# Causal masks of an attention layer: added on TensorE, or on VectorE and GpSimd

## What is computed

```python
q = (x @ wq).reshape(B, T, 2, 4, 128)          # T = 2048, 2 key groups, 4 heads each
k = einsum('bkhl,ld->bkhd', k_lat, wk_up)
scores = einsum('bqhrd,bkhd->bhrqk', q, k) * scale
scores = where(causal, scores, finfo.min)       # causal = tril(ones(T, T))
probs = softmax(scores, axis=-1)
y = einsum('bhrqk,bkhd->bqhrd', probs, v) @ wo
x = layernorm(x + y)                            # then a quantised FFN, a second
                                                # (full) attention, a mixture of experts
```

## Time and profile before

| | |
|---|---|
| median of 3 runs | 1496.16 us (1495.47 to 1496.18) |
| the profiled execution | 1495.46 us, its span 1493.7 us |
| busy: PE, DVE, ACT, POOL | 1341.5, 1087.3, 847.7, 72.0 us |
| mean granted TensorE clock | 0.924 of full speed |
| layer 0 and its FFN | from about 28 to 640 us of the span |
| layer 1 | from about 640 us to the end |

### The profile page before, as it was taken

How to read it: one execution, slowest core, us unless ns; L and a number is a source line. 1 busy time by engine, 2 the same in 40 slices (tenths; PEclk the granted TensorE clock), 3 DMA queues, 4 the chain that set the end, 5 groups by cost and what they waited for, 6 DMA issues and landing times.

```text
span 1493.7 us, 19302 instructions
## 1 busy us (share of the span) xinstructions
PE 1341.5 (90%) x6597; PEld 580.2 (39%) x6597; DVE 1087.3 (73%) x2165; ACT 847.7 (57%) x1621; POOL 72.0 (5%) x99
## 2 busy tenths in 40 slices
PE   5789899989999975789999999999999999999894
PEld 3444445344443432433333333333333333333332
DVE  3677587578644577778888788888789887987323
ACT  2445534564555421167777666777566776677660
POOL 2000000000000000000000002000011000000033
PEclk8678899899999986589999999999999999999897
DMA  3000000000000000000000000000000000000000
GB/s 100 1 1 1 1 1 1 1 1 1 1 0 1 0 1 0 0 1 1 1 1 1 1 1 8 2 1 1 1 1 8 1 1 2 1 1 1 1 7 8
DMA packets 8865, 6.19 MB, mean 4 GB/s; under 512 B 2168, under 2 KB 8128, under 8 KB 8768
## 3 DMA queue, kind: packets, MB, share of 16 engines
q1 hardware_dynamic: 8768, 4.97, 1.2%
HBM read 3.72 MB, written 1.05 MB: 3 GB/s over the span
## 4 chain that ended last, share of the span: by engine, by line
PE 72%; DVE 15%; ACT 7%; issue 3%; POOL 1%; DMA 1%; SPq 1%; DVEq 0%; POOLq 0%; ACTq 0%
PE ps L755 24%; PE ps L738 16%; PE ps L654 8%; DVE MP L1150 8%; PE ps L734 6%; PE ps L660 4%; ACT PR L932 4%; PE ps L650 2%; PE ps L719 2%; PE ps L668 1%; PE ps L686 1%; ACT QO L831 1%; PE ps L619 1%; PE ps L697 1%; POOL qc L1001 1%
## 5 line engine op out<-in xcount | busy, mean ns | idle before, releaser
L1150 DVE TENSOR_REDUCE MP<-ps 128x1 f32<-128x512 f32 (+2 forms) x1344 | 822.4, 664 | 175.8 <-PE ps L654 94.1
L932 ACT ACTIVATE PR<-ps 128x512 f32<-128x512 f32 (+2 forms) x1344 | 700.7, 586 | 438.4 <-PE ps L738 231.9
L755 PE MATMUL ps<-PR,V 128*32 128x512 f32 (+2 forms) x2688 | 438.6, 610 | 0.6 <-ACT OS L831 0.5
L738 PE MATMUL ps<-Q,KO 64*128 64x512 f32 x1024 | 364.6, 469 | 29.7 <-ACT PR L932 20.3
L654 PE MATMUL ps<-KO,Q 64*128 64x512 f32 x1024 | 353.5, 448 | 17.1 <-DVE MP L1150 12.8
L738 PEld LDWEIGHTS ps<-Q,KO 64*128 64x128 f32 x1024 | 154.9, 188 | 353.5 <-ACT PR L932 289.4
L654 PEld LDWEIGHTS ps<-KO,Q 64*128 64x128 f32 x1024 | 164.5, 192 | 82.9 <-DVE MP L1150 47.4
L734 PE MATMUL ps<-QO,KO 97*128 97x512 f32 (+3 forms) x320 | 148.5, 475 | 19.2 <-ACT PR L932 17.1
L660 PE MATMUL ps<-KO,QO 96*128 96x512 f32 (+2 forms) x320 | 137.2, 466 | 15.7 <-DVE QO L1131 12.6
L755 PEld LDWEIGHTS ps<-PR,V 128*32 128x32 f32 (+1 forms) x2688 | 74.3, 116 | 124.1 <-ACT PR L932 66.5
L734 PEld LDWEIGHTS ps<-QO,KO 97*128 97x128 f32 x320 | 63.6, 203 | 146.4 <-ACT PR L932 89.4
(11 more groups left out here) (180 smaller groups left out, 762.7 us busy)
## 6 DMA issues: line engine op xcount, KB each, us to landing
Q<-MR SPq DMA_DIRECT2D x64, 2.0 KB
result<-V SPq DMA_DIRECT2D x4, 256.0 KB, 2.3
H<-in_L_attn_wq SPq DMA_DIRECT2D x1, 512.0 KB, 6.9
HQT<-in_L_attn_wo SPq DMA_DIRECT2D x1, 512.0 KB, 4.9
ew<-in_L_ffn_expert_w SPq DMA_DIRECT2D x1, 512.0 KB
const<-in_consts SPq DMA_DIRECT2D x1, 197.0 KB, 2.3
bq<-in_L_attn_bq SPq DMA_DIRECT2D x12, 0.1 KB
wd<-in_L_ffn_w_down SPq DMA_DIRECT2D x1, 176.0 KB, 3.6
```

What stands on the lines that cost most here:

```text
L738: m = nc.tensor.matmul(dst[:, :], KO1[rows, g, kt * P:(kt + 1) * P], Q1[rows, it, h // 2, :], start=True, stop=True)
L755: nc.tensor.matmul(dst, VO[layer][:, kt, g, :], PR[:, u % NP_RING, q0:QC], start=kt == 0, stop=kt == key_tiles(layer, c) - 1).then_inc(pv_ ...
L932: nc.scalar.activation(PR[:, u % NP_RING, q0:QC], ps[:, 8 - nb + u % nb, q0:QC], ACT.Exp, scale=SCALE[layer]).then_inc(exp_done, 1)
L1150: v.tensor_reduce(MP[:, buf, h, q, kc:kc + 1], bank[:, 0:w], AX, ALU.max).then_inc(free, 1)
```

## The change

- The two mask matmuls (lines 663 and 740) are gone: 128 of each. The matmul before each now closes the bank.
- A diagonal maximum is now one `tensor_tensor_reduce` of VectorE: it adds `mask_qk` (now 512 wide, zeros and then the triangle, bf16) to the bank, writes the sum back into the bank, and keeps the maximum. The other 1216 maxima stay as they were.
- The exponents of a diagonal slot are computed unmasked. GpSimd then sets the part above the diagonal to zero in `PR` (`affine_select`, 128 by 128, in place), and the products of that slot wait for GpSimd (`clipped`) instead of ScalarE.
- The table `const` loses both masks; the one mask left comes by a DMA of its own, into `qa`, and VectorE converts it.
- The step list isn't cut any more: one walk over the whole program, with three pads at its very end, and no seam.

```diff
+        def diagonal(layer, c, kt):
+
+            return layer == 0 and kt >= c * QT
...
-            walk(part0, Count([]), 0)
-            walk(first1, n0, 0)
-            for c in range(1, NC - 1):
-                walk(padded(steps1(c, False, False)), start_of(c), HG)
-            walk(padded(steps1(NC - 1, False, True)), start_of(NC - 1), HG)
+            walk(program, Count([]), 0)
...
-            sp.dma_start(const[:, :], A["consts"]).then_inc(ld["const"], 16)
+            sp.dma_start(const[:, :], A["consts"][:, 0:CONST_W]).then_inc(ld["const"], 16)
+            sp.dma_start(qa[:, 0:P], A["consts"][:, CONST_W:]).then_inc(ld["masks"], 16)
...
                     last = nc.tensor.matmul(bank[:, 0:n], QO[0:SHIFT, buf, h, q * P:(q + 1) * P],
-                                            KO0[0:SHIFT, g, kc * QC:kc * QC + n], start=True, stop=not causal)
-                    if causal:
-                        last = nc.tensor.matmul(bank[:, n - P:n], ident_b[:, :], mask_qk[:, :], start=False, stop=True)
+                                            KO0[0:SHIFT, g, kc * QC:kc * QC + n], start=True, stop=True)
...
-                if causal:
-                    m = nc.tensor.matmul(dst[:, q0:q0 + P], ident_b[:, :], mask_kq[:, :], start=False, stop=True)
                 m.then_inc(score_full, 1)
...
-                pe.wait_ge(exp_done, n.units + u + 5)
+                if diagonal(layer, c, kt):
+                    clips_at[0] += 1
+                    pe.wait_ge(clipped, n.clips + clips_at[0])
+                else:
+                    pe.wait_ge(exp_done, n.units + u + 5)
...
+            def clip(unit, q0):
+
+                block = PR[:, unit % NP_RING, q0:q0 + P]
+                pool.wait_ge(exp_done, unit + 5)
+                nc.gpsimd.affine_select(block, block, [[1, P]], ALU.is_ge, nothing, base=0, channel_multiplier=-1).then_inc(clipped, 1)
...
+                    if layer == 0 and kc == c:
+
+                        v.tensor_tensor_reduce(bank[:, 0:w], bank[:, 0:w], mask_qk[:, QC - w:QC], 1.0, LOWEST, ALU.add, ALU.max,
+                                               MP[:, buf, h, q, kc:kc + 1]).then_inc(free, 1)
+                    else:
+                        v.tensor_reduce(MP[:, buf, h, q, kc:kc + 1], bank[:, 0:w], AX, ALU.max).then_inc(free, 1)
```

More of the change, by code:

```diff
@@ L36 @@
 NEG = -1e30
+LOWEST = -3e38
 VW0, VW1 = 64, 32
@@ L51 @@
 PAIRS = HG // 2
-CONST_W = 3 * P + 10
+CONST_W = P + 10
 def constants():
-    c = np.zeros((P, CONST_W), np.float32)
+    c = np.zeros((P, CONST_W + P), np.float32)
     i = np.arange(P)
     c[:, 0:P] = np.eye(P)
[L60 to L65, removed]
+    c[:, P:P + 4] = -0.5
+    c[:, P + 4] = (i % BAND) // HD1 == 1
+    c[:, P + 5] = (i % BAND) // HD1 == 2
+    c[:, P + 6:CONST_W] = (i % BAND == PARTS1)[:, None]
+    c[:, CONST_W:] = np.where(i[None, :] > i[:, None], NEG, 0.0)
     return c
@@ L172, in build @@
         SCORE_BANKS = (2, 3)
-        ld = {n: sem("loaded_" + n) for n in ("x", "attn0", "ffn0", "attn1", "moe", "const")}
+        ld = {n: sem("loaded_" + n) for n in ("x", "attn0", "ffn0", "attn1", "moe", "const", "masks")}
         side_full = sem("side_full")
@@ L185, in build @@
         pv_done = sem("pv_done")
+        clipped = sem("clipped")
         out_free = sem("out_free")
@@ L474, in __init__ @@
                 self.logits = kinds.count("logits")
+                self.clips = sum(s[0] == "scores" and diagonal(s[1], s[2], s[5]) for s in steps)
                 self.outs = kinds.count("out_copy")
@@ L497, in plus @@
                 return new
[L499 to L507, removed]
-        def parts(engine, walk):
-            walk(part0, Count([]), 0)
-            walk(first1, n0, 0)
-            for c in range(1, NC - 1):
-                walk(padded(steps1(c, False, False)), start_of(c), HG)
-            walk(padded(steps1(NC - 1, False, True)), start_of(NC - 1), HG)
+        program = list(steps0()) + list(steps1(0, True, False))
+        for chunk in range(1, NC):
+            program += steps1(chunk, False, chunk == NC - 1)
+        program = padded(program)
+        def parts(engine, walk):
+            walk(program, Count([]), 0)
         @block.sync
         def _(sp):
-            sp.dma_start(const[:, :], A["consts"]).then_inc(ld["const"], 16)
+            sp.dma_start(const[:, :], A["consts"][:, 0:CONST_W]).then_inc(ld["const"], 16)
+            sp.dma_start(qa[:, 0:P], A["consts"][:, CONST_W:]).then_inc(ld["masks"], 16)
             sp.dma_start(X[:, :, :], A["L0_attn_x"].rearrange("b (t p) d -> p (b t) d", p=P)).then_inc(ld["x"], 16)
@@ L728, in scores @@
                 q0 = first_query(layer, c, kt)
-                causal = layer == 0 and kt >= c * QT
                 pe.wait_ge(exp_done, n.units + 4 + max(0, u + 1 - nb))
@@ L734, in scores @@
                     m = nc.tensor.matmul(dst[:, q0:QC], KO0[:, g, kt * P:(kt + 1) * P], QO[:, buffer_of(0, it), h, q0:QC],
-                                         start=True, stop=not causal)
+                                         start=True, stop=True)
                 else:
@@ L994, in rstd @@
                 nc.gpsimd.tensor_tensor(RS[:, :], VE[:, :], minus_half, ALU.pow).then_inc(rstd_ready, 1)
+            nothing = nc.gpsimd.to_reg(0.0)
+            def clip(unit, q0):
+                block = PR[:, unit % NP_RING, q0:q0 + P]
+                pool.wait_ge(exp_done, unit + 5)
+                nc.gpsimd.affine_select(block, block, [[1, P]], ALU.is_ge, nothing, base=0, channel_multiplier=-1).then_inc(clipped, 1)
             def sum_experts(q, links):
@@ L1006, in walk @@
             def walk(steps, n, lag):
-                k, rs, tiles = 0, 0, 0
+                k, rs, tiles, units = 0, 0, 0, 0
                 for step in steps:
                     kind = step[0]
+                    if kind == "scores":
+                        if diagonal(*step[1:3], step[5]):
+                            clip(n.units + units, first_query(*step[1:3], step[5]))
+                        units += 1
                     if kind in ("y0", "y1", "down", "stats"):
@@ L1308, in _ @@
             v.tensor_copy(ident_b[:, :], ident)
-            v.tensor_copy(mask_kq[:, :], const[:, P:2 * P])
-            v.tensor_copy(mask_qk[:, :], const[:, 2 * P:3 * P])
+            dve.wait_ge(ld["masks"], 16)
+            v.memset(mask_qk[:, 0:QC - P], 0.0)
+            link(v.tensor_copy(mask_qk[:, QC - P:QC], qa[:, 0:P]))
             dve.wait_ge(ld["attn0"], 16 * 6)
```

11 lines of the change are left out of this document (4 added, 7 removed).

## The result

The changed kernel takes 1472.6 us (median of 4 executions, 1469.6 to 1475.4) against 1496.2; the ratio is 0.9844, with a 95% interval of 0.9808 to 0.9879. A second set gave 1474.1 (5 executions, 1469.9 to 1484.6), ratio 0.9877 [0.9839, 0.9916]. The profiled execution is one of the first set: 1470.66 us, span 1468.9, mean granted clock 0.929.

What follows compares the result with a forecast made beforehand. TensorE was taken as the bound late in layer 0, VectorE as often in 28 to 240 us. Masks -11, maxima +3, clips +1.5, seams -4.8, small things +0.5 sum to -10.8 us: 1485 us forecast, range 1475 to 1492, wider 1474 to 1499.

Steps and rivals of the forecast that it cites:

- the chain of work: Upper estimate for masks off TensorE: 174 of 256 masks on the path, 15.3 us; the term taken was -11 us.
- what it left out: The other 82 mask matmuls, beside a wait for VectorE or ScalarE: forecast to be worth nothing.

## What to carry to other kernels

Price a small matmul by the distance between its two neighbours, with and without it. Where only the trace with it is at hand, take the distance to the next matmul at every place, sorted by what comes next, and not one row for all: here it was 0.04 us ahead of a maximum and 0.07 to 0.16 ahead of anything else, at the full clock. Where the chain of work gives both a count and a sum for what is removed, weigh the sum: here it said 15.8 us where 15.0 +- 1.3 was measured, and what it left out was worth 0.2 +- 0.9. A view that names who ended a wait goes by the time; check that it is what the instruction waited for. And before a difference of 1% is read off a few executions, see how the time of one kernel moves with its low-clock time.

## What the runs showed that I had not expected

- The low-clock time differs between executions of one kernel without any change: 211 to 243 us of low clock in 55 executions of before, worth 0.32 us each, about 10 us of time in all.
- An add with maximum reads and writes the same PSUM bank at the rate of a plain maximum: 0.425 us for 256 columns, against 0.415 in the earlier trace rows.
- Its read-out lasts 0.139 us and adds 0.06 to 0.07 to the chain in most places.
- Setting the triangle of a 128 by 128 block to zero takes GpSimd 0.307 us, less than its addition of that size, 0.455.
